# Two-part, 32-row head stacks for the first attention, heads on alternating halves of TensorE's array, and the two score passes issued product by product in turn

## The reference

```python
q, k, v = proj(Wq, bq), proj(Wk, bk), proj(Wv, bv)      # (b, 16 heads, 256, 8)
q = q * cos + rotate_half(q) * sin;  k = k * cos + rotate_half(k) * sin
attn = softmax(einsum('bhqd,bhkd->bhqk', q, k) / sqrt(8))
x = x + (einsum('bhqk,bhkd->bhqd', attn, v) merged) @ Wo.T + bo
x = x + ffn(layernorm(x))
x = x + sparsemax_attention(layernorm(x))               # causal
x = x + ffn(layernorm(x))
```

## Time and profile before

| | |
|---|---|
| median of three runs | 669.6 us |
| profiled execution | 668.51 us, its span 666.7 us |
| PE busy | 616.4 us, 92% |
| DVE busy | 531.3 us, 80% |
| ACT busy | 386.9 us, 58% |
| POOL busy | 364.2 us, 55% |

### The profile page before, as it was taken

How to read it: one execution, slowest core, us unless ns; L and a number is a source line. 1 busy time by engine, 2 the same in 40 slices (tenths; PEclk the granted TensorE clock), 3 DMA queues, 4 the chain that set the end, 5 groups by cost and what they waited for, 6 DMA issues and landing times.

```text
span 666.7 us, 18643 instructions
## 1 busy us (share of the span) xinstructions
PE 616.4 (92%) x6534; PEld 463.6 (70%) x6534; DVE 531.3 (80%) x1547; ACT 386.9 (58%) x929; POOL 364.2 (55%) x695
## 2 busy tenths in 40 slices
PE   2569988999999999999999999999999999999894
PEld 2335545777767777766777788888788888888663
DVE  2468978899999999988788888788888888888623
ACT  1002655677777666666766656565656566666662
POOL 5643445466767666665556655465654544552322
PEclk9655999999999999999999999999999999999998
DMA  3873454554455544444554433344333243440000
GB/s 95 188 224 93 113 130 119 131 139 127 116 133 135 138 127 115 126 124 113 139 133 120 118 88 88 86 94 105 102 97 104 79 111 87 113 114 12 11 18 19
DMA packets 64750, 72.09 MB, mean 108 GB/s; under 512 B 10764, under 2 KB 58444, under 8 KB 60044
## 3 DMA queue, kind: packets, MB, share of 16 engines
q1 hardware_dynamic: 64652, 70.84, 41.9%
HBM read 46.60 MB, written 23.33 MB: 105 GB/s over the span
## 4 chain that ended last, share of the span: by engine, by line
PE 63%; DVE 15%; SPq 7%; issue 6%; POOL 3%; DMA 3%; ACT 1%; POOLq 0%; DVEq 0%; ACTq 0%
PE banks L1400 12%; PE banks L1363 7%; PE banks L1382 6%; PE banks L1366 6%; PE banks L1288 6%; PE banks L1349 6%; PE banks L1385 4%; DVE top L1038 4%; PE banks L1367 3%; PE banks L1340 3%; PE banks L1387 3%; PE banks L1341 2%; DMA k_stack<-k_image 2%; DVE f_xhat L1009 2%; SPq L766 2%
## 5 line engine op out<-in xcount | busy, mean ns | idle before, releaser
L1212 ACT ACTIVATE probs_t<-banks 128x512 f32<-128x512 f32 (+1 forms) x512 | 275.8, 551 | 167.1 <-PE banks L1387 84.5
L1032 DVE TENSOR_REDUCE neg_shift<-banks 128x2 f32<-128x512 f32 x256 | 168.0, 680 | 25.8 <-PE banks L1363 24.3
L1400 PE MATMUL banks<-probs_t,v_ext 128*32 128x256 f32 (+1 forms) x2048 | 123.8, 359 | 0.0
L1363 PE MATMUL banks<-k_stack,q_stack 72*128 72x256 bf16 x512 | 104.8, 290 | 14.1 <-issue 7.5
L1037 DVE MAX8 top<-banks 128x8 f32<-128x128 f32 x256 | 74.8, 292 | 45.7 <-PE banks L1367 42.5
L1038 DVE MAX8 top<-banks 128x8 f32<-128x256 f32 x256 | 105.9, 414 | 0.0
L908 POOL TENSOR_TENSOR hidden<-up_tanh,gate_half 128x256 f32<-128x256 f32 x96 | 68.9, 730 | 66.8 <-DVE up_tanh L1078 66.8
L1366 PE MATMUL banks<-k_stack,q_stack 72*128 72x128 bf16 (+1 forms) x512 | 100.5, 248 | 4.7 <-DVE top L1038 1.8
L1385 PE MATMUL banks<-q_stack,k_stack 75*128 75x256 bf16 (+1 forms) x512 | 100.0, 248 | 1.4 <-ACT probs_t L1212 0.9
L1382 PE MATMUL banks<-q_stack,k_stack 75*128 75x256 bf16 x512 | 99.9, 276 | 1.1 <-DMA q_stack<-neg_shift_rows 1.1
L1367 PE MATMUL banks<-mask_b,ident_b 128*128 128x128 bf16 x512 | 99.8, 220 | 0.0
(11 more groups left out here) (92 smaller groups left out, 1101.9 us busy)
## 6 DMA issues: line engine op xcount, KB each, us to landing
q_stack<-q_image SPq DMA_DIRECT2D x96, 192.0 KB
k_stack<-k_image SPq DMA_DIRECT2D x96, 192.0 KB
q_image<-qk_parts SPq DMA_DIRECT2D x32, 192.0 KB, 2.3
k_image<-qk_parts SPq DMA_DIRECT2D x32, 192.0 KB, 2.4
q_image<-qk_parts SPq DMA_DIRECT2D x32, 128.0 KB, 2.2
o_image<-out_t SPq DMA_DIRECT2D x32, 128.0 KB, 2.4
out_compact<-o_image SPq DMA_DIRECT2D x64, 32.0 KB, 2.0
rdenominators<-r_image SPq DMA_DIRECT2D x16, 128.0 KB, 2.5
```

The source lines that it names most:

```text
L1032: dve.tensor_reduce(m.nm[:, n % STACKS, h, :], scores.rearrange("p (q k) -> p q k", q=TT), AX.X, ALU.max, negate=True).then_inc(reduced, 1)
L1212: act.activation(m.pt[:, g % 2, i, 0:size], shifted_banks[:, j % 2, 0:size], ACT.Exp if is_soft(n) else ACT.Relu, scale=SCALE if is_soft(n ...
L1363: ins = pe.matmul(scores[:, qt * T:(qt + 1) * T], q, m.ks[r][0:STACK, h, :], start=True, stop=True)
L1400: ins = pe.matmul(out_bank[32 * i:32 * i + 32, at + skip:at + T], v_windows(v, kt)[:, Q * g + i, :], m.pt[:, g % 2, i, kt * T:(kt + 1) * T ...
```

## The change

For soft items q and k are split into two parts in the float32r format (float32 rounded so that TensorE multiplies it in one pass) instead of three in bf16. All four part products fit in four blocks of 8 rows, 32 rows a head; with two shift rows, 34. Even heads lie in partitions 0 to 33 of the stacks, odd heads in 64 to 97, so that a matmul uses the lower or the upper half of the array's rows. The q and k loads become four DMAs of 16 rows each instead of three of 24, the shift load two instead of one; a row is 8 KB as before. POOL's split drops one cast and one subtraction for q, for k and for the shifts. The weights' columns are reordered on the host to suit. Plain items keep their bf16 stacks, in the same memory; their first four k stacks get their rows of ones by one more DMA each.

In all items both passes' waits now stand at the head of the step, and the products of pass 1 and pass 2 alternate; dense work and pv follow. Since j and h have opposite parity, two neighbouring products in a soft step lie on opposite halves.

```diff
+HALF = 64
+SOFT_STACK = 4 * HD
+SOFT_SHIFTED = SOFT_STACK + 2
...
-    m.qs = [sb(f"q_stack{r}", [P, H, T], BF16) for r in range(STACKS)]
+    m.qs_soft = [sb(f"q_stack{r}", [P, H // 2, T], F32R) for r in range(STACKS)]
+    m.qs = [plain_view(s) for s in m.qs_soft]
...
             def load_k(n):
...
+                if is_soft(n):
+                    stack = m.ks_soft[r][:, :, :].bitcast(F32)
+                    for half in range(2):
+                        for again in range(2):
+                            first = half * HALF + again * 2 * HD
+                            sp.dma_start(stack[first:first + 2 * HD, :, :], k_soft_rows[:, half]).then_inc(k_loaded, SEM)
...
                 if is_soft(n):
+                    high, low = (m.parts_soft[:, s, which, :] for s in range(2))
                     pool.tensor_tensor(qk, m.tc[:, which, :], m.ts[:, which, :], ALU.add).then_inc(step, 1)
...
+                    pool.tensor_copy(high, qk).then_inc(step, 1)
+                    pool.wait_ge(step, base + 2)
+                    pool.tensor_tensor(low, qk, high.bitcast(F32), ALU.subtract).then_inc(done, 1)
...
+            def pass1(n, h, qt):
...
+                if is_soft(n):
+                    rows = half_rows(h, SOFT_STACK)
+                    ins = pe.matmul(scores[:, qt * T:(qt + 1) * T], m.qs_soft[r][rows, h // 2, qt * P:(qt + 1) * P],
+                                    m.ks_soft[r][rows, h // 2, :], start=True, stop=True)
...
+            def pass2(n, j, kt):
...
+                if is_soft(n):
+                    rows = half_rows(j, SOFT_SHIFTED)
+                    ins = pe.matmul(shifted[:, kt * T:(kt + 1) * T], m.ks_soft[r][rows, j // 2, kt * P:(kt + 1) * P],
+                                    m.qs_soft[r][rows, j // 2, :], start=True, stop=True)
...
+            def both_passes(step):
+
+                n, h = divmod(step, H)
+                n2, j = divmod(step - AT["pass2"], H)
+                if 0 <= n < ITEMS:
+                    begin_pass1(n, h)
+                if 0 <= n2 < ITEMS:
+                    begin_pass2(n2, j)
+                for block in range(TT):
+                    if 0 <= n < ITEMS:
+                        pass1(n, h, block)
+                    if 0 <= n2 < ITEMS:
+                        pass2(n2, j, block)
```

More of the change, by code:

```diff
@@ L736, in load_q @@
                 wait(sp, shifted_ready, (n - STACKS + 1) * H)
[L737 to L739 removed]
+                if is_soft(n):
+                    stack = m.qs_soft[r][:, :, :].bitcast(F32)
+                    for half in range(2):
+                        for again in range(2):
+                            first = half * HALF + again * 2 * HD
+                            sp.dma_start(stack[first:first + 2 * HD, :, :],
+                                         q_soft_rows[again * HD:(again + 2) * HD, half]).then_inc(q_loaded, SEM)
+                else:
+                    for rep in range(PARTS):
+                        rows = slice(rep * PARTS * HD, (rep + 1) * PARTS * HD)
+                        sp.dma_start(m.qs[r][rows, :, :], q_rows[rep * HD:(rep + PARTS) * HD]).then_inc(q_loaded, SEM)
             def load_k(n):
@@ L848, in split @@
                 qk = m.qk[:, which, :]
-                high, middle, low = (m.parts[:, s, which, :] for s in range(PARTS))
                 wait_freed(pool, "k" if which and is_soft(n) else "q", n)
                 if is_soft(n):
+                    high, low = (m.parts_soft[:, s, which, :] for s in range(2))
                     pool.tensor_tensor(qk, m.tc[:, which, :], m.ts[:, which, :], ALU.add).then_inc(step, 1)
[L853 to L862, removed]
+                    pool.wait_ge(step, base + 1)
+                    wait(pool, stored, n * each)
+                    pool.tensor_copy(high, qk).then_inc(step, 1)
+                    pool.wait_ge(step, base + 2)
+                    pool.tensor_tensor(low, qk, high.bitcast(F32), ALU.subtract).then_inc(done, 1)
+                else:
+                    high, middle, low = (m.parts[:, s, which, :] for s in range(PARTS))
+                    wait(pool, stored, n * each)
+                    pool.tensor_copy(high, qk).then_inc(step, 1)
+                    pool.wait_ge(step, base + 1)
+                    pool.tensor_tensor(qk, qk, high, ALU.subtract).then_inc(step, 1)
+                    pool.wait_ge(step, base + 2)
+                    pool.tensor_copy(middle, qk).then_inc(step, 1)
+                    pool.wait_ge(step, base + 3)
+                    pool.tensor_tensor(low, qk, middle, ALU.subtract).then_inc(done, 1)
             def split_shift(n):
```

201 lines of the change are left out of this document (130 added, 71 removed).

## The result

The changed kernel took 1186.15 us (median; 1183.35 to 1188.78), the kernel before 670.07 on the same chip: 1.769 times as long, 95% interval 1.761 to 1.777. The direction was the forecast one, the size was not, and it lies far above the range. Ratios in this document leave out executions more than 1.5% above the fastest of their kernel. The profiled execution has a span of 1181.6 us against 666.7.

A forecast was written before the change was run, and what follows sets the result against it. PE's own sequence was taken to set the pace from 60 us on. Terms +0.5 + 17 - 2.4 - 3 + 1 = +13 us on the profiled 668.5 gave 681.6, median 683; range 650 to 790.

The forecast's parts named there:

- Two halves side by side at 0.12 us a pair: Soft items: neighbouring products on opposite halves run together, a pair taking the float32r spacing of 0.12 us.
- The rival without pairing: Soft items: halves do not run side by side, +3.9 us an item, 736 us in all; chance 0.12.
- A row cut costs what a column cut costs, 0.20 in and 0.09 out: PE: assumed switch price for row cuts, 0.20 us into a float32 or float32r product, 0.09 into bf16.
- The rival of nearly free cuts: Row cuts cost almost nothing, soft items take 17.1 us instead of 18.0, median 653 us; chance 0.28.
- 64 products are 32 pairs: PE in soft items: an item's 64 pass products pair up at 0.12 us, 3.84 us instead of 7.04.
- every product switches: Soft items: 32 and 34 rows are different cuts, so each alternation pays; 882 us, or 782 without exposed loads; chance 0.27.
- Steps 256 to 284, +17 us: Overlap of plain pass 1 with soft pass 2: four switches a step, 0.58 us, times 29.
- Turns: "0 on PE", +1 us: Plain items, passes by turns: no product or switch added on PE, +1 us for 16 items, bounds 0 and +5.
- Soft item at one cut, +0.04 us: PE per soft item: pairs plus switches 8.09 us against 8.05 before, +0.5 us over 14 items.
- Switch into the rounded format, 0.20: PE: 0.09 us for the switch plus 0.11 for the weight load not loaded ahead, into a float32r product.
- POOL, -2.4 us at the start: q's and k's splits before item 0's stacks each get 1.21 us shorter, 2.4 us in all.
- k loads, -3 us: Soft items: k stacks land a little earlier, -3 us in all, bounds -5 and +11.

The follow-up runs named there:

- e1: Separate micro kernel, attention left out: series of 256-column products behind full-height ones; one cut on two halves 0.060 us a product, 32 and 34 rows by turns 0.31.
- e5: Changed kernel with a zero row ahead in each half stack (33 and 35 rows) and the passes in the order of before: 752.34 to 786.61 us.
- e10: Separate micro kernel: series of 256-column products behind 128 full-height ones; bf16 with 34 rows went from 0.109 to 0.214 us a product, 64 rows stayed at 0.109.
- e11: As e9, but both passes take 34 rows in the half of the head's parity: 727.85 us, 1.088 times the kernel before.
- e12: As e11 with 64 rows instead of 34: 706.23 us, 1.057 times the kernel before.
- e2: Changed kernel with a zero row ahead in each half stack, so the passes contract 33 and 35 rows: 779.45 us, 1.164 times the kernel before.
- e6: As e2, but products by turns only in steps below 256, then the order of before: 743.24 us median.
- e4: Kernel before with the turns alone (both waits at the head of the step, products alternating): 714.93 us, 1.068 times the kernel before.
- e9: Changed kernel, order of before, first attention's products over 72 and 75 rows of a constant tile, so no cut: 687.17 us, 1.030 times the kernel before.

## Why the prediction was wrong, step by step

- **Two halves side by side at 0.12 us a pair.** Right for one cut (e1: 0.120). The rival without pairing falls.
- **A row cut costs what a column cut costs, 0.20 in and 0.09 out.** Right: 0.30 a block. The rival of nearly free cuts falls.
- **"64 products are 32 pairs".** This is the step that failed. It took 32 and 34 rows for one cut; they are two, so all 64 products of an item switch. The rival "every product switches" had the mechanism and, at full clock, the price: 0.31 us, +14.0 us an item, 882 us. The rule of the Trainium skill behind it was right too. I gave it 0.27 and left its dearer form out of the range, although the trace showed a switch at every change of shape that it had.
- **The clock.** Named in that rival, not priced. At half clock the product is 0.51 us instead of 0.31. An estimate for an item at full clock: 17.9 - 64*0.11 + 64*0.31 is 30.7 us, with the groups' switches 32; measured 51.4. Of the 33.5 us an item gained, some 14 are the switches and 19 the clock; over 14 items 196 + 266 = 462, against 454 measured up to the last soft head. The 0.31 and the 0.51 are both seen in this kernel; the two shares stay an estimate, since no item of it ran at full clock throughout. That the clock is a cause is shown by e5. What holds it down in this kernel stays open: its products have few rows, which brought the clock down in e10 and held it down longer in e11 than in e12, and they never overlap, as in e1's series by turns, which fell as well. With 33 and 35 rows in pairs (e2) it was 1.00 from 200 to 280 us.
- **Steps 256 to 284, +17 us.** Mechanism right, size +40: the same alternation drops the clock to 0.63 there. In blocks instead of by turns it is +7 at full clock (e6).
- **Turns: "0 on PE", +1 us.** Wrong, bounds of 0 to +5 too: +47 (e4), 2.5 us a soft item and 1.3 a plain one. I had named what stood behind the two waits, but took DVE's slack of 33 us in 200 as cover. What counts is the loop from PE's product over DVE or ScalarE back to the bank: with both waits ahead, each step begins when the slower of the two loops is done.
- **Soft item at one cut, +0.04 us.** Held up to the turns: e2 and e4 both do 63 heads in 80 us, with PE busy 72.6 and 72.2 us of them, so pairs and cuts together add next to nothing there. With the passes apart a quarter pairs and the cuts cost 1.2 us an item on balance (e12 against e9).
- **Switch into the rounded format, 0.20.** Right behind pv: 0.11 dearer than with bf16 (e9). Into pv the sum had 0.09 as before; there e9 lost 0.04 more on the mean, 0.2 us an item.
- **POOL, -2.4 us at the start.** Right. The first split ends 1.94 us after it began instead of 3.10, the cast keeps its 0.40, and the first scores reach DVE at 24.98 instead of 27.42 us:

```profile
9.86 0.72 POOL L927 TENSOR_TENSOR qk<-rope_cos_terms,rope_sin_terms 128x256 f32<-128x256 f32 x1 [5.10 <-DVE rope_sin_terms L1114]
10.64 0.40 POOL L930 CAST qk_parts_soft<-qk 128x256 fp32r<-128x256 f32 x1
11.12 0.73 POOL L932 TENSOR_TENSOR qk_parts_soft<-qk,qk_parts_soft 128x256 fp32r<-128x256 f32 x1
11.80 0.73 POOL L927 TENSOR_TENSOR qk<-rope_cos_terms,rope_sin_terms 128x256 f32<-128x256 f32 x1
```

- **k loads, -3 us.** Not seen. In the changed kernel no load is near the path; in e9, where loads are as changed and PE paces, PE waits 1.5 us from 130 to 270 us, but on nothing that the profile names, against 0.4 for a k stack before. The term is not settled.

No version here beats the kernel before. What the change could give (two halves at 0.060 us a product) is less than what one block in and out costs, as long as a block holds four products: 4*(0.11 - 0.06) = 0.20 against 0.30.

## What to carry to other kernels

Ask of two neighbouring products on TensorE not whether their rows fit one half, but whether both need the same size of strip: 32 and 34 rows by turns cost 0.31 us each, while 33 and 35 start together. A padding row of zeros mended that. Before two waits are put at the head of a step, look at the loops that release them, not at the free time of the engines: one wait moved, with no product moved, cost 29 us of 668. And when a trace already shows a stretch at low clock, price every scenario at that clock too.

## What the chip showed beyond this

- TensorE can lose half its clock while it issues without a gap: 34 rows a product did it in both micro kernels (0.109 to 0.214 us bf16, 0.117 to 0.213 rounded), 64 and 66 rows did not.
- One program ran its same loop at either clock within one execution (e5: 0.50, then 1.00) and from one execution to the next came out between 752 and 787 us, e6 between 722 and 764, where the kernel before stayed within 663 to 677.
- The rounded format takes 0.120 us for 256 columns against 0.109 for bf16, and its second weight load starts 0.11 us late behind a change of cut (e1).
